# One kernel, four edits: a wait for each piece of an expert's weights, one-hot rows moved, a bank's count relaxed, a GpSimd subtraction moved

## The reference, cut to what matters

```python
# x: (8, 256, 256), after both attentions and the first feed-forward
h = layernorm(x)
scores = softmax(h @ gate_w.T).transpose(0, 2, 1)      # 16 experts
topk_w, topk_idx = top_k(scores, 32)                   # each expert takes 32 tokens of a batch
x_tok = gather(h, topk_idx)
g = x_tok @ Wg[e].T;  u = x_tok @ Wu[e].T              # 256 -> 512
eo = (gelu(g) * u) @ Wd[e].T * topk_w                  # 512 -> 256
out = scatter_add(eo, topk_idx)
shared = (gelu(h @ Ws_g.T) * (h @ Ws_u.T)) @ Ws_d.T
x = x + tanh(g_ffn[1]) * (out + shared)
```

## Time and profile before

| | us |
|---|---|
| median of 3 runs | 724.21 |
| lowest, highest | 723.71, 724.60 |
| the profiled execution, its own time | 725.76 |
| its span, first to last instruction | 723.9 |
| PE busy | 638.5 (88%) |
| DVE busy | 455.3 (63%) |
| ACT busy | 357.5 (49%) |
| POOL busy | 233.8 (32%) |

### The profile page before, as it was taken

One profiled execution on the slowest core, in us unless ns is written; L12 is line 12 of the kernel. 1 busy time (PEld: TensorE's weight loads), 2 busy tenths in 40 slices (PEclk: granted clock), 3 DMA queues, 4 the chain that ended last, 5 costly groups with the idle time before them and its releaser, 6 DMA issues.

```text
span 723.9 us, 13037 instructions
## 1 busy us (share of the span) xinstructions
PE 638.5 (88%) x4768; PEld 517.6 (71%) x4768; DVE 455.3 (63%) x931; ACT 357.5 (49%) x806; POOL 233.8 (32%) x250
## 2 busy tenths in 40 slices
PE   5889999899978778775899988999888899999997
PEld 3667666688866455543566656999776899999997
DVE  3878866111017385758676635647677777787886
ACT  3366667566643222141566766323236555665551
POOL 6655422600000510035856221000114444455510
PEclk9999999999989998996999999999999999999999
DMA  7965750790000143105767640400302366565514
GB/s 256 279 176 151 199 136 10 297 406 17 0 0 1 30 193 104 11 1 132 141 139 153 127 105 1 175 1 1 118 1 88 104 214 201 197 203 203 203 29 131
DMA packets 61637, 89.30 MB, mean 123 GB/s; under 512 B 17416, under 2 KB 50824, under 8 KB 60424
## 3 DMA queue, kind: packets, MB, share of 16 engines
q1 hardware_dynamic: 60784, 88.01, 40.2%
q10 hardware_dynamic: 800, 0.59, 0.3%
HBM read 65.64 MB, written 18.74 MB: 117 GB/s over the span
## 4 chain that ended last, share of the span: by engine, by line
PE 61%; DVE 17%; issue 8%; ACT 7%; DMA 3%; POOL 2%; SPq 1%; ACTq 0%; DVEq 0%; POOLq 0%
PE ps L1146 60%; DVE keep L2076 2%; DMA keep<-in_x 1%; DVE keep L2087 1%; ACT whi L1041 1%; SPq L515 1%; DVE att L2214 1%; DMA big<-in_wd 1%; DVE wlo L2234 1%; PE ps L1152 1%; DVE keep L2084 1%; DVE keep L2069 1%; ACT big L788 1%; ACT vp L788 1%; DVE hlo_e L2218 1%
## 5 line engine op out<-in xcount | busy, mean ns | idle before, releaser
L1146 PE MATMUL ps<-thi,whi 128*128 128x256 f32 x256 | 73.5, 287 | 8.2 <-DVE wlo L2234 5.9
L1146 PE MATMUL ps<-keep 128*128 128x120 bf16 (+8 forms) x489 | 60.6, 255 | 20.3 <-DVE keep L2076 15.2
L1146 PE MATMUL ps<-thi,wlo 128*128 128x256 f32 x256 | 72.4, 283 | 0.0
L1146 PE MATMUL ps<-tlo,whi 128*128 128x256 f32 x256 | 72.3, 282 | 0.0
L1146 PEld LDWEIGHTS ps<-keep 128*128 128x128 bf16 (+2 forms) x489 | 34.7, 112 | 41.8 <-DVE keep L2076 26.9
L914 ACT ACTIVATE ps<-ps 128x256 f32<-128x256 f32 x128 | 47.6, 372 | 34.1 <-PE ps L1146 34.0
L1026 ACT ACTIVATE att<-ps 128x512 f32<-128x512 f32 x48 | 28.6, 596 | 68.7 <-PE ps L1146 68.5
L575 POOL TENSOR_TENSOR kbr<-khi,keep 128x616 fp32r<-128x616 f32 x32 | 40.0, 1271 | 63.1 <-PE ps L1146 60.8
L1146 PEld LDWEIGHTS ps<-thi,whi 128*128 128x128 f32 x256 | 48.7, 190 | 10.8 <-issue 5.5
L1146 PE MATMUL ps<-xhi,phi 128*128 128x512 f32 x128 | 50.8, 397 | 2.9 <-ACT ps L914 2.9
L1146 PE MATMUL ps<-xhi,plo 128*128 128x512 f32 x128 | 50.3, 393 | 0.0
(11 more groups left out here) (259 smaller groups left out, 1857.3 us busy)
## 6 DMA issues: line engine op xcount, KB each, us to landing
q_rows<-qhi SPq DMA_DIRECT2D x32, 256.0 KB, 2.7
big<-in_piw SPq DMA_DIRECT2D x4, 2048.0 KB, 13.5
qpair<-q_rows SPq DMA_DIRECT2D x8, 768.0 KB, 5.5
qhead<-q_rows SPq DMA_DIRECT2D x8, 768.0 KB, 7.6
q_rows<-qlo SPq DMA_DIRECT2D x16, 256.0 KB, 2.9
att<-in_wg SPq DMA_DIRECT2D x8, 512.0 KB, 3.9
att<-in_wu SPq DMA_DIRECT2D x8, 512.0 KB, 4.8
att<-in_wd SPq DMA_DIRECT2D x8, 512.0 KB, 5.6
```

What stands on the lines that cost most here:

```text
L1146: return pe.matmul(out, lhsT, rhs, start=start, stop=stop, skip_group_check=True)
```

## The change

Four edits, which add and remove no arithmetic.

1. `gate_up` gets `split_from`: for half 0 of an expert TensorE waits for the low part of piece 0 ahead of m = 0 and for that of piece 1 ahead of m = 1, and no longer for both ahead of the first matmul.
2. VectorE makes the one-hot rows of batches 4 and 5 ahead of the low parts of expert 0's tokens, and those of batches 0, 1 and 2 one expert earlier, ahead of the first low part of expert 5, 9 and 13.
3. The last down waits until down 13 is emptied (`emptied`), whose bank it writes, not until down 14 is; and five moved combinations go ahead of the last groups where four did.
4. GpSimd makes the low part of piece 2 of expert 0 right after the third norm of the dispatch, not after the eighth.

```diff
@@ GpSimd @@
                 pool.wait_ge(nhi_done, b + 1)
                 pool.tensor_tensor(nlo[b % 3], xn_all[:, 2 * b:2 * b + 2, :], nhi[b % 3], ALU.subtract
                                    ).then_inc(nlo_done, 1)
+                if b == 2:
+                    pool.wait_ge(d_hi, 1)
+                    pool.tensor_tensor(wlo[0][:, PIECES[2]], raw[0][:, PIECES[2]], whi[0][:, PIECES[2]],
+                                       ALU.subtract).then_inc(d_split, 1)
...
-            for q in range(4):
-                low_parts(0, q, True)
+            for q in range(1, 4):
+                low_parts(0, q)
@@ TensorE @@
-            def gate_up(u, f, slot, tokens, first=False):
+            def gate_up(u, f, slot, tokens, first=False, split_from=None):
                 if not first:
                     pe.wait_ge(h_done, u * 2 + (f - 1))
                 for m in range(2):
+                    if split_from is not None:
+                        pe.wait_ge(gu_split, split_from + m)
...
-            def down(u, s, slot, h, first=False):
+            def down(u, s, slot, h, first=False, emptied=None):
                 pe.wait_ge(h_done, u * 2 + 2)
                 if not first:
-                    pe.wait_ge(down_done, u)
+                    pe.wait_ge(down_done, u if emptied is None else emptied)
...
-                    pe.wait_ge(gu_split, t * 8 + (2 * q + 2))
...
-                    gate_up(u, 0, s, tokens)
+                    gate_up(u, 0, s, tokens, split_from=t * 8 + (2 * q + 1))
...
             pe.wait_ge(d_split, E)
-            down(B + E - 1, 1, 1, (hhi_e, hlo_e))
+            down(B + E - 1, 1, 1, (hhi_e, hlo_e), emptied=B + E - 2)
...
-            for b in range(4):
+            for b in range(5):
                 combine_moved(b)
             for b in range(B):
-                if b >= 4:
+                if b >= 5:
                     combine_moved(b)
@@ VectorE @@
             for b in range(2, B):
                 slots_one_hot(b)
+            rows_of_slots(4)
+            rows_of_slots(5)
             for c in range(DC):
                 dve.wait_ge(t_hi, c + 1)
                 dve.tensor_tensor(tlo[0][:, S * c:S * c + S], XT[:, 0, c, :], words(thi[0])[:, S * c:S * c + S],
                                   ALU.subtract).then_inc(g_done, 1)
-            rows_of_slots(4)
-            rows_of_slots(5)
...
                 for s in range(2):
+                    if s == 0 and t in (2, 4, 6):
+                        rows_of_slots(t // 2 - 1)
                     for f in range(2):
...
-                    if s == 0 and t in (2, 4, 6):
-                        rows_of_slots(t // 2 - 1)
```

More of the change, by code:

```diff
@@ L709, in _, with low_parts @@
                                    ).then_inc(nlo_done, 1)
-            def low_parts(t, q, first):
+                if b == 2:
+                    pool.wait_ge(d_hi, 1)
+                    pool.tensor_tensor(wlo[0][:, PIECES[2]], raw[0][:, PIECES[2]], whi[0][:, PIECES[2]],
+                                       ALU.subtract).then_inc(d_split, 1)
+            def low_parts(t, q):
                 x, slot = t * 4 + q, q % 2
-                if not (first and q == 0):
-                    pool.wait_ge(t_hi, x + 2)
-                    pool.tensor_tensor(tlo[slot], XT[:, bass.ds(x, 1), :, :].rearrange("p o c t -> p (o c t)"),
-                                       thi[slot], ALU.subtract).then_inc(t_split, 1)
+                pool.wait_ge(t_hi, x + 2)
+                pool.tensor_tensor(tlo[slot], XT[:, bass.ds(x, 1), :, :].rearrange("p o c t -> p (o c t)"),
+                                   thi[slot], ALU.subtract).then_inc(t_split, 1)
                 pool.wait_ge(d_hi, x + 1)
@@ L720, in low_parts @@
                                    ALU.subtract).then_inc(d_split, 1)
-            for q in range(4):
-                low_parts(0, q, True)
+            for q in range(1, 4):
+                low_parts(0, q)
             with pool.Fori(1, E // 4) as t:
                 for q in range(4):
-                    low_parts(t, q, False)
+                    low_parts(t, q)
         @block.scalar
```

## The result

| | before | changed |
|---|---|---|
| median of 20 runs, us | 724.43 | 727.33 |
| lowest, highest | 722.35, 726.57 | 723.41, 733.45 |
| the profiled execution, its own time | 725.76 | 733.45 |
| its span | 723.9 | 731.6 |

The changed kernel is slower: its time is 1.0035 times the other's, with a 95% interval of 1.0018 to 1.0051, and 2.9 us lie between the medians. The prediction had 723.9 us, with 718.5 to 726.5 around it, and was wrong: the measured time lies above that.

The account below looks back on a forecast made before the run. The prediction took TensorE, 61% of the chain, as the bound, so only closing gaps between matmuls pays. Gains of 10.5 us less costs of 10.2 gave a median of 723.9 us, range 718.5 to 726.5.

Parts of the forecast that it names:

- part 4: GpSimd's subtraction moved ahead of the dispatch: gain 2.0 us at the last dispatch, cost 2.2 before the shared down.
- the turn: VectorE and GpSimd operations in SBUF exclude one another, the waiting engine goes next; losing it costs 2.3 us behind 1024 columns.
- Part 1: Experts' starts: the split wait ends eight waits for weights' low parts, gain 6.2 us; activations' low half is late next.
- Part 2: One-hot rows ahead of expert 0's tokens: the 1.78 us gap at expert 1 goes, the 1.16 one stays; gain 1.2.
- Part 3: Other one-hot rows one expert earlier: turns lost near expert 4 and in 9 and 13, cost 7.8 us.
- Part 5: Last down: it starts at once, gain 1.3 us, less small gaps in the last groups; net 1.1, between 0.5 and 1.5.
- A cast loses its turn as well: Rival: GpSimd's request precedes VectorE's cast, waits about 4.0 us, not 2.7; one 725.3 to 726.2, both 727.6; slow ones 0.23.

Follow-up runs that it names:

- no4: The changed kernel without edit 4, so with edits 1, 2 and 3; 724.95 us, ratio 1.0013 to the kernel before.
- hold4: The changed kernel with GpSimd's moved subtraction made to wait until the last shared activations are made; 724.59 us, ratio 0.9992 to the kernel before.
- only1: The kernel before with edit 1 alone, the wait for each piece; 730.08 us, ratio 1.0074.
- hold4_rows: hold4 with the one-hot rows of batches 0, 1 and 2 back after experts 4, 8 and 12; 726.15 us, ratio 1.0030 to the kernel before.
- only4: The kernel before with edit 4 alone, GpSimd's subtraction moved ahead of the dispatch; 727.57 us, ratio 1.0039.

## Why the prediction was wrong, point by point

**The step that failed is in part 4.** It priced the moved subtraction by the turn alone, "cost 2.2", and said "The bounds are 0 and 2.4". The wait itself came out as forecast: some 4 us before the shared down, 3.75 in the trace, 2.0 more than before. But the bounds held no term for what a TensorE that is idle this long does next. Its granted clock fell to 0.50 in each of the four profiles with a wait of 3.7 to 3.9 us at this place, and in none of the nine with 1.73; the 24 matmuls took 4.6 to 5.5 us where 3.1 is usual. That is 1.5 to 2.4 us more, on top of the 2.0, and it decided the sign.

The trace of before had shown it, in a place that I had not read. Its granted clock by windows:

```profile
510.00:512.00 2.00, 1.58 (x8) 1.52 (x9) 1.86 (x5) 0.00 (x0) 0.11 (x1) 0.55 0.05 8
512.00:514.00 2.00, 2.00 (x13) 2.00 (x13) 1.81 (x5) 0.00 (x0) 0.00 (x0) 0.60 0.77 246
```

This is right behind the wait of 2.8 us at the routing, the longest in the edited stage. By the Trainium skill (TensorE: Matmul & The Clock Gate, Part 1) a gate passes fewer clock pulses when TensorE has not been busy of late; the trace agrees, with 5.5 us for 24 matmuls behind 3.75 us of idleness.

**The same term in the experts.** A lost turn is a wait of 1.8 us, and behind some of these the clock falls too: over all profiles, 8 of the 27 waits of 1.76 to 2.28 us in the experts (23 are lost turns, four are waits for a low part at expert 1), at 1.6 us where I could measure it (216 matmuls in 27.95 and in 26.35 us). None of the shorter waits in the experts, up to 1.56 us, was followed by it, nor any of the nine of 1.70 to 1.74 at a dispatch. What decides between the 8 and the other 19 stays open. So an edit that trades eight short waits for four long ones loses by it, even where the sum of idle time is equal.

**Part 1** was right: no wait for the low parts of weights, and what was late next was the low half of the activations, by GpSimd's turn.

**Part 2**, gain 1.2: 1.78 and 1.16 became one of 1.82, 1.1 of idle and 0.2 for the gap, 1.3. Right in mechanism and size.

**Part 3**, three lost turns, 7.8: three came, at experts 4, 7 and 13 where near 4, 9 and 13 were forecast, at 1.8 of idle and 0.2 each, 6.0. The size was 1.8 too high: at expert 4 the low half ended at 598.91 + 2.81 = 601.72, 1.9 us after TensorE was ready (599.95 - 0.16), where I had put 14.0 - 11.52 = 2.5. The mechanism, rows that push the cast into GpSimd's request, is right by no4 and hold4, which lost their turns at experts 5, 9 and 13 behind the rows; in the changed kernel's profile only the one at 13 is theirs, and 4 and 7 came with late weights. What was wrong is to charge it to the move: with the rows at their old place edit 1 loses as many turns (only1, hold4_rows).

**Part 4's gain**, 2.0 at the last dispatch: the wait of 1.74 is gone. Right.

**Part 5**, net 1.1: the 1.02 is gone and two gaps of 0.22 and 0.25 stand at the end, against 0.14 and 0.22 before; 0.9 of idle and 0.2. Right.

**The sum.** Without the clock the stretch would be 1.9 us shorter (2.1 less 4.0) where the sum had 0.3, and what lies between them is the lost turns that I overrated. So the terms that stood in the sum were right to 1.6 us together, in the kernel's favour, and the one that was missing came to 4.0 in the profiled execution. By the medians edit 4 alone costs 2.9 us (only4) and the other three 0.3 (no4). Edit 4's own terms are 2.0 of wait and 1.5 to 2.4 of clock, less 2.0 at the last dispatch: 1.5 to 2.4. The 0.5 to 1.4 between that and 2.9 I have not placed; the interval of only4, 0.5 to 5.1 us, holds both, and by only4's mean granted clock part of it can be clock lost elsewhere.

**The rivals.** "A cast loses its turn as well" did not happen in the changed kernel, but did in edit 1 alone. My chance for slower, 0.23, rested on it, and the time that it named, 727.6, is close to the measured one for a reason that has nothing to do with it.

## What to carry to other kernels

Price a wait of TensorE by its length, not only by its sum: behind a wait of about 1.8 us or more, look for the matmuls at half pace in the windows of the profile, and add them to the term. Before an edit makes the bottleneck engine earlier, list which operations of VectorE and GpSimd will then meet, and hold the one with slack behind a semaphore that the urgent one raises: here one line of waiting was worth 8.5 us to edit 1. Test a bundle of edits apart: here three of them together came to nothing, one lost 2.9 us, and the one that looked like the gain lost 5.2 by itself.

## What the hardware showed that I had not expected

- At the routing's wait of 2.8 us, the same in all kernels, the clock fell in 11 of 14 profiles and did not in three; from there to the end of the next wait, 114 matmuls and transposes, took 14.5 or 14.6 us with the fall and 13.1 without. So one kernel's executions differ by such falls, and two single profiles can differ by several us with no edit between them.
- The start of the edited stage moved by 10.4 us over 14 profiles (505.63 to 515.98) of kernels that are the same up to there. The mean granted clock moved with the time: 0.958 in the execution of 733.45 us, 0.983 in that of 716.44. I did not find what makes one execution lose the clock earlier than another; no run was made for it.
- Whether a turn is lost is decided by about 0.1 to 0.3 us: at 570.56 against a cast from 570.33 to 570.76, and a low half then waits for the whole of GpSimd's operation, 2.75 in place of 0.69.
